# Second edge stage of a graph network: DVE's wait for gathers one leaky step earlier, scale ahead of a leaky step

## The reference, cut to what matters

```
agg = segment_sum(x[src] * w, dst)
out = leaky(x * agg @ W1 + b1) + leaky(agg @ W2 + b2)
x   = layernorm(x + out / norm(out))

msg = gelu(gelu(x[dst] @ W1p + b1p) @ W2p + b2p) * w
agg = segment_sum(msg, src)
h   = gelu(gelu([x, agg] @ W1u + b1u) @ W2u + b2u)
x   = layernorm(x + h / norm(h))
```

## Time and profile before

| what | value |
|---|---|
| three runs | 3011.1, 3018.17 and 3018.83 us, median 3018.17 |
| profiled execution | 3019.24 us in all, span 3017.4 us |
| PE busy | 2161.6 us, 72% of the span |
| DVE busy | 2204.7 us, 73% |
| ACT busy | 1066.6 us, 35% |
| POOL busy | 2383.8 us, 79% |
| DMA moved | 516.47 MB, mean 171 GB/s |
| mean granted TensorE clock | 0.762 of full speed |

### The profile page before, as it was taken

How to read it: one execution, slowest core, us unless ns; L and a number is a source line. 1 busy time by engine, 2 the same in 40 slices (tenths; PEclk the granted TensorE clock), 3 DMA queues, 4 the chain that set the end, 5 groups by cost and what they waited for, 6 DMA issues and landing times. The chain is left out here.

```text
span 3017.4 us, 39223 instructions
## 1 busy us (share of the span) xinstructions
PE 2161.6 (72%) x11956; PEld 1702.2 (56%) x11956; DVE 2204.7 (73%) x5529; ACT 1066.6 (35%) x1964; POOL 2383.8 (79%) x1774
## 2 busy tenths in 40 slices
PE   3046555555554553279898989989989998699997
PEld 3035555455454553257676666667667766466664
DVE  5079988888888886368777777777777777288888
ACT  0000000000000000045444444445445454288887
POOL 7678888888888888658888888888888887488888
PEclk8555555555555555589999999999999999699998
DMA  9898888888887766467776777776777676356664
GB/s 229 203 208 191 171 174 180 180 182 175 170 183 166 157 147 138 71 179 180 172 176 162 170 175 167 164 175 164 172 171 175 159 175 136 83 192 207 208 206 157
DMA packets 1036086, 516.47 MB, mean 171 GB/s; under 512 B 540544, under 2 KB 998336, under 8 KB 1035880
## 3 DMA queue, kind: packets, MB, share of 16 engines
q1 hardware_dynamic: 764616, 372.57, 47.1%
q0 software_dynamic: 144256, 77.17, 18.4%
q10 hardware_dynamic: 127008, 64.23, 7.5%
HBM read 269.97 MB, written 243.84 MB: 170 GB/s over the span
## 5 line engine op out<-in xcount | busy, mean ns | idle before, releaser
L300 PE MATMUL sums<-xg,weigh 128*128 128x64 f32 x1960 | 435.0, 418 | 518.0 <-ACT ms L323 380.9
L544 POOL DMA_INDIRECT state<-ms,sidx x392 | 657.2, 1677 | 157.4 <-issue 114.3
L256 POOL DMA_INDIRECT table<-ms,sidx x392 | 622.5, 1588 | 140.9 <-issue 115.2
L300 PEld LDWEIGHTS sums<-xg,weigh 128*128 128x128 f32 x1960 | 420.5, 327 | 551.7 <-issue 485.1
L368 DVE TENSOR_SCALAR weigh<-rowp,key,ew 128x128 f32<-128x128 f32 (+3 forms) x784 | 424.0, 603 | 167.7 <-PE rowp L288 160.1
L530 POOL DMA_INDIRECT box<-table,node_dst x392 | 397.7, 1015 | 128.6 <-issue 112.8
L243 POOL DMA_INDIRECT xg<-in_x,node_src x392 | 383.1, 977 | 120.8 <-issue 104.6
L323 ACT ACTIVATE ms<-sums 128x256 f32<-128x256 f32 x98 | 37.6, 384 | 1143.1 <-DMA table<-ms,sidx 1057.6
L374 DVE SCALAR_TENSOR_TENSOR seen<-rowp,key,earlier 128x128 f32<-128x128 f32 (+3 forms) x784 | 383.3, 544 | 0.0
L735 DVE SCALAR_TENSOR_TENSOR leaky<-z_p,bz,leaky 128x512 f32<-128x512 f32 x294 | 219.7, 748 | 212.4 <-ACT leaky L656 210.1
L577 PE MATMUL z_p<-turned_s,wz 128*128 128x512 f32 x588 | 325.9, 638 | 2.8 <-DVE leaky L735 1.6
(11 more groups left out here) (93 smaller groups left out, 3553.4 us busy)
## 6 DMA issues: line engine op xcount, KB each, us to landing
box<-table SPq DMA_DIRECT2D x97, 768.0 KB, 5.0
joins<-weigh ACTq DMA_DIRECT2D x98, 640.0 KB, 3.8
weigh_in<-joins SPq DMA_DIRECT2D x98, 640.0 KB, 6.8
table<-rows SPq DMA_DIRECT2D x97, 512.0 KB, 5.3
pair<-state SPq DMA_DIRECT2D x97, 512.0 KB, 3.9
xin<-in_x SPq DMA_DIRECT2D x97, 256.0 KB, 6.1
state<-y SPq DMA_DIRECT2D x97, 256.0 KB
out<-y SPq DMA_DIRECT2D x97, 256.0 KB, 2.2
```

The costliest lines, as they stand in the source:

```text
L256: pool.indirect_dma_start(out=table[:, :], out_offset=bass.IndirectOffsetOnAxis(ap=sidx[0][:, i:i + 1], axis=0), in_=ms[k % MR][:, b, :], ...
L300: last = pe.matmul(sums[k % 2][:, a * D:(a + 1) * D], block_of(0, k, b)[:, a * P:(a + 1) * P], xg[:, k * WT + b, :], start=b == a, stop=b ...
L544: pool.indirect_dma_start(out=state[:, :], out_offset=bass.IndirectOffsetOnAxis(ap=sidx[1][:, at:at + 1], axis=0), in_=ms[k % SM][:, b, :] ...
```

## The change

The two waits that stood in front of the product (all four gathers of the window landed, and the plain load landed) get a function of their own, `arrive`. It stands in DVE's round ahead of leaky step 2, while the product stays at the end of the round. The scale moves from behind leaky step 1 to in front of it. No instruction of another engine is changed.

```
-                        def multiply(i):
+                        def arrive(i):
 
                             s = i % SB
                             dve.wait_ge(gathered[s], 16 * WT * (i // SB + 1))
                             dve.wait_ge(loaded[s], 16 * (i // SB + 1))
+
+                        def multiply(i):
+
+                            s = i % SB
                             dve.tensor_tensor(box[s][:, :, 1, :], box[s][:, :, 1, :], box[s][:, :, 0, :], ALU.mult).then_inc(multiplied, 1)
...
                             of(t, 1, leak, 0)
+                            of(t, 2, scale)
                             of(t, 1, leak, 1)
-                            of(t, 2, scale)
+                            of(t, 0, arrive)
                             of(t, 1, leak, 2)
                             of(t, 3, normalize)
                             of(t, 2, add_rows)
```

## The result

| | before | after |
|---|---|---|
| median of seven runs | 3019.55 us (3011.1 to 3022.64) | 3028.62 us (3025.2 to 3032.6) |
| profiled execution, in all and span | 3019.24, 3017.4 us | 3025.2, 3023.5 us |

The ratio is 1.0032, with a 95% interval of 1.0021 to 1.0044: slower by 0.3%. The forecast was 3003 us. The direction was wrong, the time lies inside the range.

The account below looks back on a forecast made before the run. POOL's back-to-back issues were taken to bound the kernel at 13.21 us a round. Holds falling from 0.56 to 0.38 over 86 rounds (15.5 us) plus 1 at the start gave 16.5 less: 3003 us, range 2974 to 3044.

Parts of the forecast that it names:

- Its root: Second edge stage: POOL's pace is 12.65 us a round plus holds, and scatters do not wait for ACT.
- (a): DVE's list: no instruction is added or removed; the product's two waits stand one leaky step earlier.
- (b): Scale ahead of leaky step 1: off the path, only hastens the stage's first scatter, 1 us gain (bounds 0 and 1.7).
- (c): DVE after the gathers land: leaky step 2, normalization, addition, product in a row, the product 2.41 us after landing.
- (d): SP's queue: box loads start 4.3 us after the gathers instead of 0.1, costing POOL nothing directly.
- the creep: Gathers: a late landing delays the addition, hence the next burst and landing, up to some 3 to 5 us.
- rival 3: First scatters wait for scatter 4's landing, over 4.7 us; half the rounds pay 1.0; +27 us, 3046; chance 0.16.
- (e): POOL's holds: normalization, addition, product in a row make nearly one hold a round, 0.38 us on average instead of 0.56.
- Rival 2: Landing 0.1 us sooner, product just ahead of scatter 3: POOL held 0.8 every round, +21 us, 3040; chance 0.10.
- Rival 1: Gathers' landing stays at 1.76 us, product starts behind scatter 3's issue: almost no hold, 2972; chance 0.15.
- Rival 5: The port lock holds DVE too: its three operations wait out POOL issues; period 14.1, +77 us, 3096; chance 0.02.

Follow-up runs that it names:

- the repeated run: The changed kernel run again, unchanged, beside the kernel before on another occasion: ratio to before 1.0037.
- the version that beats both: The changed kernel with SP's box load also waiting for gathers landed three windows before, and one small unused sum ahead of the product: 2989.37 us, 0.9901.
- The run with early loads: The changed kernel with SP's box load released by ScalarE's last slope of window i-4 instead of the addition of window i-6: ratio to before 0.9959.
- the one-operand product: The kernel before with the product replaced by a TENSOR_SCALAR by 1.0, its multiplication left out: ratio to before 0.9951.
- the one-operand row: The changed kernel with the box load at the gathers' landing and normalization, addition and product replaced by TENSOR_SCALAR by 1.0: ratio to before 0.9843.

## Why the prediction was wrong

- **Its root** held: POOL sets the pace, and the period is 12.65 + holds + stall. Scatters waited for ACT once in 1200 us.
- **(a), (b)**: the first scatter came 1.1 us earlier (57.12 to 56.04 behind the first gather), forecast 1. That is no proof, since two kernels with DVE's old order and another wait of SP came at 55.95 and 56.13. Not foreseen was that the scale brings a hold onto the last gather when it is moved alone.
- **(c)** held: the product stands 2.40 us behind the landing, forecast 2.41. The granted clock fell as was allowed for, and hardly reached POOL. Here are the stretches from 1430 to 2540 us (length; busy us of PE, PEld, DVE, ACT, POOL; granted clock as a share of 2.4 GHz; DMA share; GB/s), before and after:

```profile
1430.00:2540.00 1110.00, 1003.34 (x6058) 767.04 (x6056) 802.71 (x1765) 551.47 (x1008) 905.17 (x673) 0.94 0.73 169
```

```profile
1430.00:2540.00 1110.00, 1042.24 (x5988) 819.12 (x5988) 811.59 (x1745) 544.60 (x996) 884.11 (x667) 0.88 0.72 167
```

  PE is busier by 39 us for no more work: it ran at the lower of its two levels more often. The output products alone took 294.6 us instead of 244.2, behind 62 us of idle time for leaky step 2 instead of 25. In the round at 2013.89 above, 24 output products behind an idle time of 1.71 us took 4.67 us; the granted clock was 0.67 from 2014 to 2016 us and 0.50 from there to 2020.
- **(d)** is the step that failed. Right was that SP's queue moves: L499 stood 0.1 to 4.0 us behind the gathers' issue (median 1.3), and now stands 4.2 to 7.2 behind it (median 4.7). Wrong was the sentence "This costs POOL nothing directly." The same burst also lies around the fourth scatter, whose landing the next first scatter must have. It took over 4.7 us in 50 of 86 rounds: 0.27 us a round, 23 us, a term that the sum has at nothing. Wrong too was the creep: the landings of gathers, expected at 3 to 5 us, stayed at 1.76 us in the median (1.72 before), over 3 us in 12 rounds of 86. That mattered, because the creep was the argument against rival 3, which has this stall with its place and its condition, and about twice its price (half the rounds at 1.0, +0.5; measured 48 rounds at 0.48, +0.27 on the mean). Rival 3 got 0.16 because I argued that a crept landing takes L499 behind scatter 4's packets. By the table this needs L499 within 1 us of the end of that issue; it stood at 3.3 us in the median.
- **(e)** has the right number, 0.385 us of holds against 0.38 (0.45 in the repeated run), and in part by luck. Forecast was nearly one hold a round, with no phase locked. There are 61 in 86 rounds, of 0.53 us on the mean, none in 25 rounds, and 42 of them are on the third scatter.
- **Rival 2**, the lost tie, happened in 10 rounds of 86 (as at 2015.52), for 0.77 us each, 0.09 us a round; it was to be every round. (Its text has the product 0.06 us ahead of scatter 3; from its own 4.17, 0.1 and 4.11 that is 0.04.) **Rival 1** needs no stall and no hold; the version that beats both comes nearest (0.25 us of holds, no stall). **Rival 5** is refuted for this kernel's operations: those of DVE inside POOL's issues kept their 0.95 us.

With the stall put in, the prediction's own sum reads -16.5 + 22.9 = +6.4 us; the spans differ by 6.1. The run with early loads says the same from the other side: it has 0.21 us a round less of stall and about the same holds, which is 0.6% of the time, and its ratio is 0.7% lower.

Open: which DMA queue's packets delay a scatter's landing inside the burst. The load (L499), the joins (L504) and the store (L509) go out together in every kernel here, and were not separated. Nor was a kernel without the joins' load tried.

## What to carry to other kernels

For an engine that issues back to back, write the round as undisturbed issues + holds + stalls; a change of another engine's order can only work through the last two, and each can be read from the trace. When a wait moves, follow the semaphores raised behind it to the DMAs that they release, and check the landing of every transfer that shares the time, not only the one in view: here the gain in holds was real and the moved load took back more. Place such a load by its phase in the round of the engine that it can delay: a load issued 10 us later cured the stall. The cure was one wait more on SP, which put the load between the two landings that matter.

## What the runs showed of the hardware

**What holds POOL.** An indirect DMA of POOL behaves as if it asked, 0.13 us into its issue, for something that certain DVE operations own, and is then held until the running one ends. From 1430 to 2540 us of before, every hold over 0.08 us (123 of 123) ends with a TENSOR_TENSOR of two SBUF operands, within 0.06 us; in the changed kernel 58 of 58. Over the traces of before, after and the one-operand product in this stretch, operations that had started at least 0.07 us before the issue and ended at least 0.1 us behind its request held POOL as follows: normalization, product and addition in every case (54, 53 and 11 in before); the 0.56 us TENSOR_SCALAR in 9 of 9; leaky steps and the scale, which take one operand from PSUM, never (290 and 57 cases); TENSOR_REDUCE never (108). The Trainium skill, "SBUF — State Buffer" (Who interferes with whom), says that a DVE instruction contends with a GpSimd instruction that reads SBUF if it has two SBUF inputs, with GpSimd if it runs in a 2-port mode, that one with at most one SBUF input outside these modes does not, and that on this chip a reduction never does. The traces agree for three of the kinds, and for the TENSOR_SCALAR if its 0.56 us are a 2-port mode, which no trace names.

**Who is held depends on the kind.** A two-operand operation that starts inside a POOL issue keeps its 0.95 us (252 in the stage before, 0.95 to 0.96 us; 239 in the stage after, at most 0.99). The fast one-operand form doesn't always. Three rows of the timeline of the one-operand row:

```profile
1707.71 1.58 POOL L546 DMA_INDIRECT state<-ms,sidx  x1 [0.30 <-issue]
1707.79 0.55 DVE L786 TENSOR_SCALAR y<-y 128x768 f32<-128x768 f32 x1
1708.26 0.90 DVE L782 TENSOR_SCALAR y<-y 128x768 f32<-128x768 f32 x1
```

The second lasts 0.90 instead of 0.55 us and ends at 1709.16, 0.13 before the issue's end. Of this kernel's three one-operand calculations, 42 were stretched beyond 0.65 us from 1430 to 2540, and all 42 end 0.13 to 0.15 us before a scatter's issue does. In turn POOL is held where such an operation runs over the end that an issue would have had: 12 of the 18 holds here have no operation over the request and end 0.08 to 0.09 us behind a TENSOR_SCALAR. With the one-operand product 8 of 74 holds go on past the normalization that ran over the request, and end in the same way. The same section of the Trainium skill lets whichever is first have the ports for the whole instruction and blocks the other fully. For the fast form something like it is seen, over the last part of an issue; for two-operand operations only POOL is held, which is why rival 5 failed.

**How sharp the tie is.** Over the twelve traces without one-operand forms, from 1430 to 2540 us, a two-operand DVE operation of the row that started 0.04 to 0.20 us ahead of an issue held it by over 0.4 us in 214 of 214 cases, one 0.02 to 0.04 us ahead in 32 of 34, and one 0.00 to 0.02 us ahead in 1 of 32; none that started 0.00 to 0.12 us behind it did (210 cases).

**Landing of a small scatter under plain transfers.** In the six traces of the table, a median of 1.6 us when the first of three plain transfers (768 + 640 + 256 KB) was issued 7 to 8 us before the end of its issue, and of 5.4 us when it was issued 1 to 2 us before (17 rounds); 3.5 us when that was in the last microsecond (11 rounds).
